# A decoder layer on one core: two token tiles of the output projection of self-attention are started before P times V of the last head pair

## The reference

```python
q = (x @ wq).reshape(B, S, 16, 64)          # k and v likewise
scores = einsum('bqhd,bkhd->bhqk', q, k) + bias
weights = softmax(scores)
context = einsum('bhqk,bkhd->bqhd', weights, v).reshape(B, S, 1024)
x = layernorm(x + context @ wo)
```

## Time and profile before

| | us |
|---|---|
| median of three runs | 4514.3 |
| lowest and highest run | 4512.64, 4514.62 |
| profiled execution, own time | 4509.74 |
| its span, first to last instruction | 4507.9 |
| mean granted TensorE clock (1 is full) | 0.95 |

### The profile page before, as it was taken

The page is one execution under the profiler, slowest core; times in us unless marked ns, Lnnn a source line. Parts: engine busy times, 40 slices in busy tenths (PEclk is TensorE's granted clock), DMA queues, the critical chain, the costliest instruction groups (busy, mean ns, idle before and its releaser), DMA issues. The chain is left out here.

```text
span 4507.9 us, 90480 instructions
## 1 busy us (share of the span) xinstructions
PE 3896.7 (86%) x36730; PEld 2344.8 (52%) x36730; DVE 2494.0 (55%) x4793; ACT 1579.7 (35%) x3181; POOL 905.4 (20%) x1012
## 2 busy tenths in 40 slices
PE   5999887889998878899988788999987829999992
PEld 3767444547674445476643454766535504444441
DVE  3777335767773357577733676777236762222224
ACT  2444125744441257344413573444136700000000
POOL 2333101113330011133300112333001102222220
PEclk8999998999999999999999899999998969999996
DMA  8333258633332686333326853333178514444545
GB/s 261 93 88 88 85 222 297 207 110 88 88 88 85 240 294 201 101 88 93 83 85 260 287 188 101 94 92 93 71 281 282 171 59 106 127 123 110 139 112 168
DMA packets 285607, 659.36 MB, mean 146 GB/s; under 512 B 23920, under 2 KB 90144, under 8 KB 281968
## 3 DMA queue, kind: packets, MB, share of 16 engines
q1 hardware_dynamic: 269776, 616.08, 42.4%
q0 software_dynamic: 15120, 35.46, 4.1%
q10 hardware_dynamic: 320, 2.23, 0.1%
HBM read 384.84 MB, written 210.11 MB: 132 GB/s over the span
## 5 line engine op out<-in xcount | busy, mean ns | idle before, releaser
L493 ACT ACTIVATE sc<-sc,nmax 128x1024 f32<-128x1024 f32 x512 | 586.9, 1147 | 774.0 <-DVE nmax L712 773.2
L457 POOL TENSOR_SCALAR sc<-sc,pinv 128x1024 f32<-128x1024 f32 x512 | 574.6, 1122 | 1254.4 <-DVE pinv L720 1242.4
L824 DVE CUSTOM_DVE_ANT_0 sc<-psum,big 128x896 f32<-128x896 f32 (+7 forms) x512 | 373.4, 748 | 215.3 <-PE psum L1163 177.1
L988 PE MATMUL psum<-pts,wct 32*64 32x256 f32 x8192 | 465.6, 381 | 28.2 <-PEq L983 28.2
L988 PE MATMUL psum<-xall,wct 32*64 32x256 f32 x8192 | 466.1, 381 | 0.0
L962 PE MATMUL psum<-xt,w_all 128*128 128x256 f32 x1792 | 415.7, 385 | 15.6 <-PEq L959 15.6
L493 ACT ACTIVATE sc<-sc,xmax 128x896 f32<-128x896 f32 (+7 forms) x512 | 394.4, 772 | 70.0 <-DVE xmax L824 64.9
L730 DVE STREAM_TRANSPOSE pts<-sc 128x1024 f32<-128x1024 f32 (+3 forms) x352 | 333.0, 946 | 135.4 <-PE psum L988 92.4
L962 PEld LDWEIGHTS psum<-xt,w_all 128*128 128x128 f32 x1792 | 332.5, 190 | 120.4 <-issue 56.0
L988 PEld LDWEIGHTS psum<-pts,wct 32*64 32x64 f32 x8192 | 312.2, 134 | 131.2 <-issue 75.2
L712 DVE CUSTOM_DVE_ANT_0 sc<-psum,table_a 128x1024 f32<-128x1024 f32 x256 | 309.3, 1208 | 123.3 <-PE psum L972 106.3
(11 more groups left out here) (158 smaller groups left out, 5580.6 us busy)
## 6 DMA issues: line engine op xcount, KB each, us to landing
wct<-xall SPq DMA_DIRECT2D x576, 128.0 KB, 2.4
big<-skew_d SPq DMA_DIRECT2D x48, 1024.0 KB, 5.4
w_sb<-w_dram SPq DMA_DIRECT2D x48, 1024.0 KB, 6.3
big<-skew_d SPq DMA_DIRECT2D x48, 768.0 KB, 4.4
big<-skew_d SPq DMA_DIRECT2D x32, 896.0 KB, 4.6
big<-skew_d SPq DMA_DIRECT2D x32, 640.0 KB, 5.3
w_all<-wqkv_dram SPq DMA_DIRECT2D x33, 512.0 KB, 3.5
skew_d<-wct SPq DMA_DIRECT2D x8, 2048.0 KB, 6.9
```

Source lines behind the costliest of these rows:

```text
L457: pool.tensor_scalar(sc[k % 4][:, :], sc[k % 4][:, :], pinv[:, k % 4:k % 4 + 1], 1.0, ALU.mult, ALU.mult).then_inc(probs_scaled, 1)
L493: act.activation(tile, tile, ACT.Exp, bias=least, scale=-1.0, accum_out=total).then_inc(probs_ready, 1)
L824: dve.tensor_tensor_reduce(scx[u % 2][:, at], SCORES[:, at], skw[u % 4][:, at], -XSCALE, BIG, ALU.add, ALU.min, xmax[:, k:k + 1]).then_inc ...
L988: mm = pe.matmul(OSUM[HEAD[h], a, :], v_all[rows, ST * (b % GROUPS) + b // GROUPS, HEAD[h]], ptf[h][rows, QG * b:QG * b + QG], start=(b == ...
```

## The change

A new function `open_wo` on PE stands in the last pair between the scores of the last tile and P times V. It waits for `wo`, then multiplies for token tiles 0 and 1 (`EARLY = 2`) the first seven chunks, in halves of 256 columns, into the four `SPARE` halves. After P times V the two tiles get one product each, of the eighth chunk, in banks 0 and 1, and DVE adds both parts to `xr`. The projection uses banks 0 to 3 in turn, and PE waits for the add of the tile four before. The load of `wo` is issued ahead of the 16 spreads of the last pair.

```diff
--- before.py
+++ after.py
@@ -41,6 +41,7 @@
 QG = 2 * P
 PARTS = 12
 WEIGHED = (0, 16, 24, 32)
+EARLY = 2
 TABLE_PARTS = {3: [(S + 3 * P, TOEP)], 6: [(S, S + 3 * P)], 7: [(S - P, S), (0, S - P)]}
 GROUPS = P // DH
 KB = S // DH
@@ -296,10 +297,12 @@
                 sp.dma_start(w_all[:, 2 * DC * P:3 * DC * P], wqkv[hp, :, 2 * DC * P:3 * DC * P]
                              ).then_inc(wv_loaded, 16)
 
-            def spread_v():
+            def spread_v(last=False):
 
                 sp.wait_ge(v_copied, 1)
                 sp.sem_inc(v_copied, -1)
+                if last:
+                    sp.dma_start(wo_sb, wo.rearrange("(c p) n -> p c n", p=P)).then_inc(wo_loaded, 16)
                 for c in range(GROUPS):
                     for a in range(GROUPS):
                         sp.dma_start(v_all[DH * a:DH * a + DH, ST * c:ST * c + ST, :], vt[DH * c:DH * c + DH, :, :]
@@ -351,8 +354,7 @@
                     load_wv(hp + 1)
                     next_table(hp + 1, 6)
                     next_table(hp + 1, 7)
-                spread_v()
-                sp.dma_start(wo_sb, wo.rearrange("(c p) n -> p c n", p=P)).then_inc(wo_loaded, 16)
+                spread_v(last=True)
 
                 def load_wx(qd, free=None, uses=1):
 
@@ -775,8 +777,11 @@
                 dve.sem_inc(xr_loaded, -16)
                 for t in range(ST):
                     dve.wait_ge(y_ready, t + 1)
-                    done(dve.tensor_tensor(xr[:, t, :], SLOT[t % 2][:, 0:D], xr[:, t, :], ALU.add))
+                    done(dve.tensor_tensor(xr[:, t, :], psum[:, t % 4, :], xr[:, t, :], ALU.add))
                     dve.sem_inc(y_added, 1)
+                    if t < EARLY:
+                        row = xr[:, t, :].rearrange("p (a n) -> p a n", a=2)
+                        done(dve.tensor_tensor(row, psum[:, 4 + 2 * t:6 + 2 * t, QG:2 * QG], row, ALU.add))
                     ins = dve.bn_stats(stats[:, t, :], xr[:, t, :])
                 done(ins)
                 dve.sem_inc(y_ready, -ST)
@@ -989,6 +994,16 @@
                                                ptf[h][rows, QG * b:QG * b + QG], start=(b == 0), stop=(b == KB - 1))
                     mm.then_inc((part_weighed, part_weighed, o_ready)[part], 1)
 
+                def open_wo():
+
+                    pe.wait_ge(wo_loaded, 16)
+                    pe.sem_inc(wo_loaded, -16)
+                    for i in range(2 * EARLY):
+                        t, n = i // 2, i % 2
+                        for c in range(IC - 1):
+                            pe.matmul(SPARE[i], big[:, c, P * t:P * t + P], wo_sb[:, c, QG * n:QG * n + QG],
+                                      start=(c == 0), stop=(c == IC - 2))
+
                 def attend(which, first=False, more=True):
 
                     def fill(vs, parts=()):
@@ -1018,6 +1033,8 @@
                     fill((), (3, 4))
                     score(7, which)
                     fill((), (5, 6, 7))
+                    if not more:
+                        open_wo()
                     pe.wait_ge(slot_read, TP)
                     pe.sem_inc(slot_read, -TP)
                     if more:
@@ -1049,14 +1066,13 @@
                 pe.wait_ge(o_taken, 1)
                 pe.sem_inc(o_taken, -1)
                 pe.sem_inc(ct_free, 1)
-                pe.wait_ge(wo_loaded, 16)
-                pe.sem_inc(wo_loaded, -16)
                 for t in range(ST):
-                    if t >= 2:
-                        pe.wait_ge(y_added, t - 1)
-                    for c in range(IC):
-                        mm = pe.matmul(SLOT[t % 2][:, 0:D], big[:, c, P * t:P * t + P], wo_sb[:, c, :],
-                                       start=(c == 0), stop=(c == IC - 1))
+                    if t >= 4:
+                        pe.wait_ge(y_added, t - 3)
+                    first = IC - 1 if t < EARLY else 0
+                    for c in range(first, IC):
+                        mm = pe.matmul(psum[:, t % 4, :], big[:, c, P * t:P * t + P], wo_sb[:, c, :],
+                                       start=(c == first), stop=(c == IC - 1))
                     mm.then_inc(y_ready, 1)
 
                 def evacuated(r):
```

## The result

The changed kernel takes 4493.4 us (median of 6 runs), the kernel before 4513.7 (median of 6 on the same chip). The ratio is 0.9956, with a 95% interval of 0.9943 to 0.9968: faster by 20.3 us, where 33.6 were forecast. The profiled execution took 4493.31 us, 16.4 less than that of before (4509.74), and its span is 4491.5.

What follows compares the result with a forecast made beforehand. PE, busy 86% of the span, was taken to bound the kernel, with an idle hole before P times V. Gains of 28.2 and 9.85 less 2.4 and 2.1 gave 33.6 us: 4514.3 to 4480.7 us, range 4470 to 4496.

Steps and rivals of the forecast that it cites:

- The hole: PE idle between last scores and P times V, about 7 us per batch; early products fill it all: 28.2 us gained.
- The clock of P times V: P times V, formerly at half clock at first, runs at full clock after unbroken PE work: 9.85 us gained.
- The clock of the early products: Early products behind the scores start at low clock in batches 1 and 4: 2.4 us lost, bounds 0 to 11.4.
- their halving: Early products as 56 instructions of 256 columns instead of 28 of 512: 0.52 us per batch, 2.1 us lost in all.
- the sum: All terms over four batches: 28.2 + 9.85 - 2.4 - 2.1 = 33.6 us gained.
- the third rival: Later stages, with their own clock, hand time back: some 5 us; all back means 4514; handed back or unseen: chance 0.06.
- Weights, spreads, DVE: Before P times V, weights land at 472.9, spreads by 485.3, hidden; at projection start, DVE's second adds, 0.9 us each, hidden.
- The rival's price for being late: Weights mix evenly with spreads, early products start at 485.3: 15 us lost, 4529 us; chance of slower 0.04.
- Four banks: In the output projection, four banks in turn spare PE a wait for DVE; cost and gain 0.

Runs made afterwards that it cites:

- warm16: Kernel before plus 16 useless products between last scores and P times V, and 192 semaphore increments in the output projection: 4514.9 us, ratio 0.9999.
- early1: Changed kernel with 200 semaphore increments more per batch and one early token tile instead of two: 4485.8 us, ratio 0.9937.
- late: Changed kernel with the load of wo issued behind the 16 spreads, as before the change: 4528.7 us, ratio 1.0030.
- pad56: Kernel before plus 56 semaphore increments per batch on PE's list in the output projection: 4528.7 us, ratio 1.0032.
- bridge0: Changed kernel with the first seven products of token tile 2 ahead of the wait for ACT's copy of the last output: 4489.7 us, ratio 0.9940.

## Why the prediction was right in kind, and what it missed

- **The hole.** Right: 28.2 us of idle time forecast and found gone, in all batches.
- **The clock of P times V.** Right in size: from its start to the projection 73.4 us became 63.2, 10.2 less, forecast 9.85. The reason was incomplete. It said that the clock alone decides; warm16 and early1 show that at full clock P times V can also stand still, by all signs for want of instructions, and all but three short stops came in these two, the only kernels in which P times V begins at full clock while the DMA engines are still busy. The second tile happened to see to this.
- **The clock of the early products and their halving.** The 56 instructions took 50.9 us in all instead of the 48.1 that left the end, so these two terms cost 2.8 us together, forecast 4.5. At full clock one takes 0.216 us, not the 0.224 of the earlier trace rows, which leaves 0.3 us for the halving (2.1 forecast) and 2.5 for the rest, in the main the clock (2.4 forecast, though spread over other batches).
- **The scores ahead.** A term the sum did not have. The last scores stood at the low clock for longer, 14.5 us instead of 10.3. They are the same instructions in the same place. Their sum is 11.8 in late, 12.7 in warm16 and 13.0 to 14.9 in the others, so the kernel before had a lucky profile rather than the changed one a bad one. I count it as the clock's own variation, for which the third rival allowed 5 us; no run tested it.
- **Weights, spreads, DVE.** Right: landed at 473.3 (472.9 forecast), spreads at 482.2 (485.3 at the latest by the forecast) and hidden, adds hidden. late shows that the order of the two loads decides. The rival's price for being late was too high in its own stretch (a loss of 15 us forecast, 1.7 measured), because the weights came at 482.6 and not at 485.3: with 9.3 us again from their own issue, they did not mix with the spreads.
- **Four banks.** Right: 1.4 us.
- **The step that failed** is the third rival's: "That all 33 us are given back would need a load that arrives at a fixed time; the only one close by, the context". I looked for what can hand time back among the kernel's own loads, and at starting times. What handed back 9 of them was neither: it was PE's instruction list, 56 entries longer, whose 16 KB transfer now lies inside a store that is waited for. With the borders put back the kernel takes 4481.3 us, near the sum's 4480.7, if in part by luck. The instruction row in the queue table of the page was there to be read; the sum treated added instructions as costing only what they take on PE.
- **Left open:** 4.7 us in the cross-attention scores. They are there in the changed kernel and in late (834.4 and 833.8 us), less so in pad56 (831.6) and bridge0 (830.4), and the other kernels lie between 827.6 and 830.9. So the packet is not clearly their cause. Of the 13.3 us between the forecast gain (33.6) and the measured one (20.3), the place behind the last scores gives -2.0 (35.6 instead of 33.6), the scores +4.2, the stage behind +9.2, cross-attention +4.7, all else +1.1, and -3.9 is that the profiled execution of before lies 3.9 us from its median and that of after 0.1, a distance that the prediction kept constant.

## What to carry to other kernels

An idle stretch of PE is best filled with work that is due later anyway, and the operands of that work must be issued ahead of what is queued there; here the order of two loads was worth as much as the whole change won. When instructions are added to or taken from a list, look in the packet records for where the instruction transfers fall before and after, and at whether one lies inside a transfer that something waits for: a kernel that is slower for no visible reason in an untouched stage may be cured by a few instructions that do nothing. A comparison of two versions should therefore be made with the borders held in place, or a gain or loss of 0.3% may be that of the borders.

## What the runs showed of the hardware

- An instruction transfer of 16 KB (256 of PE's instructions) takes 0.9 to 1.9 us beside the 2 MB store, on one of the 16 DMA engines that carry the data, and the store then lands 0.8 to 2.0 us later (7.6 to 8.8 us after its issue instead of 6.8 to 6.9). With the clock that falls in the longer wait this cost the changed kernel up to 3.4 us per batch at one place. Per execution, kernels that differ in the place of the border alone lie 12 to 14 us apart.
- P times V in tiles of 32 rows uses up 75 instructions per us at full clock. Where it began at full clock while loads kept the DMA engines busy, it stopped at a distance of 256 instructions or a multiple of it (0.4 to 2.0 us from one matmul to the next); at the low clock, as in the kernel before, no such stop is seen.
- One DMA of 2 MB in the same queue and ahead of sixteen others was slowed little by them (9.6 to 10.3 us in the four batches, 8.7 to 9.3 when issued behind them), while they went from 2.4 to 8.4 us each (medians).
